# One pair of heads in eight is clipped, squared and summed on ScalarE, and a copy of scores stands ahead of the joint root

## The reference, cut to what matters

```python
def entmax15(x):
    x = (x - jnp.max(x, -1, keepdims=True)) / 2.0
    xs = jnp.flip(jnp.sort(x, -1), -1)
    rho = jnp.arange(1, x.shape[-1] + 1, dtype=x.dtype)
    mean = jnp.cumsum(xs, -1) / rho
    meansq = jnp.cumsum(xs * xs, -1) / rho
    ss = rho * (meansq - jnp.square(mean))
    tau = mean - jnp.sqrt(jnp.clip((1.0 - ss) / rho, 0.0, None))
    support = jnp.sum(tau <= xs, -1, keepdims=True)
    tau_star = jnp.take_along_axis(tau, support - 1, -1)
    return jnp.square(jnp.clip(x - tau_star, 0.0, None))
...
for _ in range(NUM_STEPS):                       # 3
    scores = jnp.einsum('bhsd,hnd->bhsn', xi, K) * beta
    w = entmax15(scores)
    xi = jnp.einsum('bhsn,hnd->bhsd', w, V)
```

## Time and profile before

| | us |
|---|---|
| median of 3 runs | 1895.13 |
| fastest and slowest of them | 1890.72, 1898.94 |
| the profiled execution, its own time | 1889.23 |
| its span, first to last instruction | 1887.4 |
| the Hopfield stage within the span | about 700 to 1382 |
| one beat in the steady part | 24.3 to 25.9 |
| one beat with output products | 26.7 to 33.6 |

### The profile page before, as it was taken

The page is one execution under the profiler, slowest core; times in us unless marked ns, Lnnn a source line. Parts: engine busy times, 40 slices in busy tenths (PEclk is TensorE's granted clock), DMA queues, the critical chain, the costliest instruction groups (busy, mean ns, idle before and its releaser), DMA issues. The chain is left out here.

```text
span 1887.4 us, 31938 instructions
## 1 busy us (share of the span) xinstructions
PE 1669.1 (88%) x10554; PEld 1156.6 (61%) x10554; DVE 1469.5 (78%) x3080; ACT 1234.6 (65%) x2769; POOL 699.6 (37%) x1326
## 2 busy tenths in 40 slices
PE   4959899999999888788889997888886899997999
PEld 3537544444444577577768886677764455545888
DVE  7767789999997268999997969999446789826655
ACT  3633477888777534788986768888652588865322
POOL 2001222222222215666675646666232111224632
PEclk9979799999999899888889999989987799988999
DMA  3464143233330100000000000000038223110000
GB/s 123 140 217 68 35 75 86 52 59 69 69 69 2 45 1 1 1 1 1 1 1 1 1 1 1 1 1 1 1 105 191 44 54 67 36 58 18 13 12 23
DMA packets 36996, 82.27 MB, mean 44 GB/s; under 512 B 9952, under 2 KB 12384, under 8 KB 35936
## 3 DMA queue, kind: packets, MB, share of 16 engines
q1 hardware_dynamic: 36192, 78.65, 17.0%
q10 hardware_dynamic: 640, 1.57, 0.4%
HBM read 52.53 MB, written 27.26 MB: 42 GB/s over the span
## 5 line engine op out<-in xcount | busy, mean ns | idle before, releaser
L1167 ACT ACTIVATE probs<-pss 128x512 f32<-128x512 f32 (+3 forms) x1152 | 481.6, 495 | 129.0 <-PE pss L1130 127.9
L873 DVE TENSOR_REDUCE negmax<-px 128x2 f32<-128x1024 f32 (+2 forms) x480 | 508.5, 1113 | 45.0 <-PE px L855 42.1
L1730 POOL TENSOR_SCALAR rp<-sw,tau 128x256 f32<-128x256 f32 x720 | 343.0, 512 | 7.1
L1234 POOL TENSOR_SCALAR_AFFINE_SELECT probs<-probs 128x512 f32<-128x512 f32 x192 | 120.8, 637 | 506.1 <-ACT probs L1167 506.1
L1130 PE MATMUL pss<-queries,keys 64*128 64x512 f32 (+3 forms) x1152 | 295.9, 396 | 5.6 <-ACT probs L1167 4.3
L855 PE MATMUL px<-keys,queries 63*128 63x512 f32 (+3 forms) x1152 | 266.3, 418 | 10.5 <-DVE negmax L873 10.5
L1130 PEld LDWEIGHTS pss<-queries,keys 64*128 64x128 f32 x1152 | 167.5, 191 | 152.5 <-ACT probs L1167 134.7
L1144 PE MATMUL po<-probs,vals 128*32 128x512 f32 (+3 forms) x2304 | 248.7, 508 | 0.4 <-POOL probs L1234 0.2
L1585 PE MATMUL pss<-again,sw 128*128 128x256 f32 x1024 | 248.9, 402 | 0.0
L1887 DVE BATCH_NORM_STATS2 st<-rp 128x6 f32<-128x512 f32 x360 | 229.6, 675 | 0.9 <-POOL rp L1730 0.9
L1585 PEld LDWEIGHTS pss<-again,sw 128*128 128x128 f32 x1024 | 206.6, 206 | 29.9
(11 more groups left out here) (375 smaller groups left out, 2548.1 us busy)
## 6 DMA issues: line engine op xcount, KB each, us to landing
queries<-rec_q SPq DMA_DIRECT2D x92, 128.0 KB, 3.6
keys<-rec_k SPq DMA_DIRECT2D x92, 128.0 KB, 3.6
queries<-rec_q SPq DMA_DIRECT2D x92, 64.0 KB, 3.4
keys<-rec_k SPq DMA_DIRECT2D x92, 64.0 KB, 3.4
rec_q<-fs SPq DMA_DIRECT2D x16, 256.0 KB, 4.2
rec_k<-fs SPq DMA_DIRECT2D x16, 256.0 KB, 4.4
rec_q<-vals SPq DMA_DIRECT2D x16, 256.0 KB, 3.0
rec_k<-vals SPq DMA_DIRECT2D x16, 256.0 KB, 3.6
```

The source lines that it names most:

```text
L873: return e.tensor_reduce(out, from_px, X_AXIS, ALU.max, negate=True)
L1167: e.activation(tl.probs[arg][:, w, :], tl.pss[scores % 3][:, 512 - width:512], ACT.Exp).then_inc(self.exp_made, 1)
L1730: x = e.tensor_scalar(self.rp[rp % 6][:, :, h], self.view(g, q)[:, h, :], -BIG, self.tau[r][:, 2 * q + h:2 * q + h + 1], ALU.min, ALU.max)
```

## The change

One pair of heads per round, pair 0 (`WHOLE` = 1), gets its two sums on ScalarE: for each of its two heads one ACTIVATE clips 256 scores and adds them up on the way (`accum_out`, into the place where `bn_stats` would have put the mean), and a second squares the result and adds that up (into `z`). Pair 1 is clipped on ScalarE and read by VectorE as before. `BY_ACT` falls from 3 to 2, so GpSimd clips pairs 2 to 7, six instead of five. VectorE has 7 `bn_stats` per round instead of 8, waits for the totals (`totals_made`) at the start of the first and of the joint step, and scales the totals by 1/256 in one small instruction of each. The ring `ra` shrinks from 7 buffers to 5. In ScalarE's order the copy `c` now stands ahead of the joint root `J`, and the first root `r` ahead of a cut and a square.

```diff
-    BY_ACT = 3
-    ACT_ORDER, PE_ORDER = "Jcdtttstsrt2ss1ttastsbss0", "ttttatbtttxcdR"
+    WHOLE, BY_ACT = 1, 2
+    ACT_ORDER, PE_ORDER = "cJdtttsrtst2ss1ttastsbss0", "ttttatbtttxcdR"
...
+        def totals(g, r):
+
+            nonlocal whole
+            self.wait_negated(e, g, r)
+            par = (g + 1 + r) % 2
+            if whole:
+                e.wait_ge(self.totals_made, whole)
+            for h in range(2):
+                e.activation(self.ends_at[h][:], self.view(g, 0)[:, h, :], ACT.Relu, bias=self.negated(g, r)[:, h:h + 1],
+                             accum_out=self.st[par][:, r, 0, 3 * h + 1:3 * h + 2]).then_inc(self.clipped, 1)
+            for h in range(2):
+                e.wait_ge(self.clipped, 2 * (whole // 2) + h + 1)
+                e.activation(self.square[h][:], self.ends_at[h][:], ACT.Square,
+                             accum_out=self.z[par][:, r, h:h + 1]).then_inc(self.totals_made, 1)
+            whole += 2
...
-                for q in range(self.BY_ACT):
+                for q in range(self.WHOLE, self.BY_ACT):
                     relus(g, r, q, ra)
                     ra += 1
+                totals(g, r)
...
-    def first_step(self, e, g, step, read_a, read_p):
+    def first_step(self, e, g, step, read_a, read_p, totals):
...
+        e.wait_ge(self.totals_made, totals)
+        step(e.tensor_scalar(m[:, whole], m[:, whole], 1.0 / NM, None, ALU.mult))
         at = step(e.tensor_tensor(m[:, by_pool], m[:, by_pool], neg[:, by_pool], ALU.add))
...
-        e.scalar_tensor_tensor(z, m2, 256.0, st[:, :, 2], ALU.mult, ALU.add).then_inc(self.first_asked, 1)
+        e.scalar_tensor_tensor(z[:, parts], m2[:, parts], 256.0, st[:, parts, 2], ALU.mult,
+                               ALU.add).then_inc(self.first_asked, 1)
...
-    def joint_step(self, e, beat, step, read_a, read_p):
+    def joint_step(self, e, beat, step, read_a, read_p, totals):
...
+        e.wait_ge(self.totals_made, totals)
+        step(e.tensor_scalar(m[:, :, whole], m[:, :, whole], 1.0 / NM, None, ALU.mult))
...
         def moments(g, r, between):
             st = self.st[(g + 1 + r) % 2][:, r]
-            pool, act = range(self.BY_ACT, self.PAIRS), range(self.BY_ACT)
+            pool, act = range(self.BY_ACT, self.PAIRS), range(self.WHOLE, self.BY_ACT)
```

27 lines of the change are left out of this document (17 added, 10 removed).

## The result

| | us |
|---|---|
| before, median of 20 runs on the same chips | 1893.59 (1885.73 to 1898.94) |
| after, median of 20 runs | 1899.53 (1892.53 to 1908.0) |
| ratio | 1.0033, 95% interval 1.0021 to 1.0046 |
| the same changed kernel in a later set of runs (`after_again`) | 1900.01; ratio 1.0048 (1.0029 to 1.0067) |
| profiled execution of after, its own time | 1899.79 |

They are not the quotient of the two medians and can differ from it by 0.1%.

A forecast was written before the change was run, and what follows sets the result against it. The loop of ScalarE's chain plus TensorE matmuls was taken to bound steady beats, VectorE close behind. Steady -0.4, c ahead of J +4.4, filling +1.2, emptying -1.0 gave +4.2 us; on the 1895.1 median, 1899.3 us, range 1888 to 1911.

The forecast's parts named there:

- s: Cost of adding up per ACTIVATE on ScalarE: 0.10 us taken, bounds 0 and 0.21; a round +0.12 us.
- The square of 256: ScalarE's ACTIVATE squaring 256 scores: claimed to go at 0.265 us before the cost of adding up.
- rival of the dear sum: ScalarE rounds 2 and 1: adding up near 0.21 us lengthens steady beats by 1.12; sum +15.6, 1910.7 us; chance 0.24.
- counterpart at s = 0: Steady beats if adding up costs nothing: a round -0.28 us, sum about -6 us; range end 1893.
- The loop: ScalarE's cuts, squares, clipping of rounds 2 and 1, TensorE's last turn, scores c and d, copy of d: 23.99 us.
- VectorE's hold on the steady beats: VectorE's thresholds delay ScalarE's cuts by 3.2 us in 15 beats, the most a faster VectorE could give.
- forecast -0.4: Sum over 15 steady beats: ScalarE's longer rounds cost 2.2 and 0.6 us, against 3.2 no longer held by VectorE.
- GpSimd: Six pairs clipped, VectorE waits for rp; its loop 23.0 to 23.9 us, still below the loop through ScalarE.
- c ahead of J: Three beats where c waits for the output product: J and the cuts come later, 1.3 + 1.3 + 1.75, +4.4 us.
- Fill: Second beat, J queued behind c, thresholds at 751.7 in place of 750.6, plus GpSimd's longer round: +1.2 us.
- Tail: Beat of 1294.8, no scores left: 1.5 of VectorE's 2.25 us hold falls away, output products take part back: -1.0 us.
- a fallen clock in the product beats: Rival: TensorE's clock falls in three beats with products, up to +8 us on top of +4.2, 1907; chance 0.07.

The follow-up runs named there:

- vector_spared: Kernel before with pair 2's bn_stats left out each round, a copy of pair 0's six numbers in its place: 1880.58 us, ratio 0.9953.
- r_early_only: Kernel before with only the first root r moved one cut and one square earlier: 1885.34 us, ratio 0.9975.
- r_late: Changed kernel with the first root r back behind the second square, c still ahead of J: 1895.64 us, ratio 1.0026.
- no_adding_up: Changed kernel without accum_out totals, pair 0 taking pair 1's sums: 1895.04 us, ratio 1.002.
- c_first_only: Kernel before with only copy c moved ahead of the joint root J: 1895.98 us, ratio 1.0024.
- experiment 11: The run r_late: changed kernel with the first root r back behind the second square: 1895.64 us, ratio 1.0026.
- plain_out_of_the_loop: Kernel before's J-first order, r early; ScalarE clips two plain pairs in rounds 2 and 1, one whole and three plain in round 0: 1880.78 us, ratio 0.9932.
- three_pairs_and_whole: Changed kernel with BY_ACT 3: ScalarE clips one whole and two plain pairs, GpSimd five: 1947.78 us, ratio 1.0305.
- c_first_where_free: Changed kernel with J ahead of c in the second beat and four product beats, c ahead of J elsewhere: 1891.96 us, ratio 1.0001.
- j_first: Changed kernel with the joint root J ahead of copy c again in every beat: 1893.55 us, ratio 1.0014.

## Why the prediction was right, and where it was not

**The price of adding up (right).** s was taken at 0.10 from the pace of a small root, with bounds 0 and 0.21. It is 0.09. No row tied a root to a total, so that the two are so close is luck; the bounds were the sound part. The square of 256 was put too low, 0.265 for 0.31; it had been worked out as a difference of two others that read PSUM, and this one reads SBUF, which may be the reason; no run separates it. Together a round costs +0.16 and not +0.12. The estimates worked out from the figures of the Trainium skill (ScalarE: Activation LUTs, What ACT_TABLE_LOAD costs), 0.400 and 0.306, agree with the 0.40 and 0.31 that the rows show for clip and square. The rival of the dear sum fell with this. (Its counterpart at s = 0 was added up wrongly: 9 x 2 x -0.28 + 0.6 - 3.2 is -7.6 and not -6. That moves the 1893 to about 1892, inside the stated range.) The Trainium skill's rule to clip on VectorE (ScalarE: Activation LUTs, Rules for kernel authors) was not put to a test: no run here clips there.

**The loop (right).** It said: cuts, squares, two rounds, last turn, c and d, copy of d, 23.99 us in the earlier trace rows, and the thresholds behind it. The floor is 23.87 (`vector_spared`), and the rest follows from the length of a round: 23.87 + 2 x 0.16 = 24.19, measured 24.19 to 24.30 in eleven of fourteen steady beats; 23.87 + 2 x (0.16 + 0.81) = 25.8 with one more pair, measured 25.9 where the clock held. The second of these decides: a loop through GpSimd is 24.2 us long too (below), but with one more pair on ScalarE GpSimd has one less.

**VectorE's hold on the steady beats (term too small).** The prediction added up ScalarE's waits for the thresholds, 3.2 us in 15 beats, and called this the most that a faster VectorE could give. `r_early_only` took 6.2 us off 14 steady beats, `vector_spared` 8.0. A wait at one place shows only what is left of a delay when it gets there. The prediction counted ScalarE's waits for turns, 2.5 us, as TensorE's own; in `vector_spared`, where only VectorE was relieved, they are gone from all fourteen beats. TensorE's clock stood higher there as well (0.98 in the first seven beats, 0.86 before), so it is not shown how much of them was VectorE's doing at first hand; and of the 8.2 us the waits for thresholds are 3.6 and those for turns 2.6 in these fourteen beats, so that some 2 us stand in neither. The right measure was the beat itself against its floor, (171.9 + 170.5) / 14 - 23.87 = 0.59 us a beat, 8.2 in all. It did no harm here, because the whole pair gave back 14 x 0.32 = 4.5 of it: steady beats came out 2.0 us better (2.9 in the second profile), forecast -0.4 in one more beat.

**GpSimd (right in kind, its loop put too short).** Twelve clippings take 5.7 to 5.9 us and VectorE waits for `rp`, 0.25 twice in a beat; less than the 0.5 to 1 us that was foretold. A wait that was not foretold is the larger one, 0.8 us for the one plain pair of ScalarE at the start of round 1, whose clipping follows two squares. In `r_late` the steady beats are as long, and VectorE stands before L1820 instead. VectorE's timeline from the start of round 1 to the thresholds:

```profile
1164.15 0.69 DVE L1909 BATCH_NORM_STATS2 st<-ra 128x6 f32<-128x512 f32 x1 [0.83 <-ACT ra L1642]
1164.76 2.46 DVE L1913 BATCH_NORM_STATS2 st<-rp 128x6 f32<-128x512 f32 x4
1167.48 0.69 DVE L1913 BATCH_NORM_STATS2 st<-rp 128x6 f32<-128x512 f32 x1 [0.26 <-POOL rp L1749]
1168.40 0.69 DVE L1913 BATCH_NORM_STATS2 st<-rp 128x6 f32<-128x512 f32 x1 [0.23 <-POOL rp L1749]
...
1178.50 0.17 DVE L1892 SCALAR_TENSOR_TENSOR neg<-step,neg 128x32 f32<-128x32 f32 x1
```

GpSimd's timeline of that beat, its start behind the thresholds and its round 1:

```profile
1154.58 0.20 POOL L1738 TENSOR_SCALAR tau<-neg 128x16 f32<-128x16 f32 x1 [4.50 <-DVE neg L1892]
...
1162.70 5.67 POOL L1749 TENSOR_SCALAR rp<-sw,tau 128x256 f32<-128x256 f32 x12
```

Between these rows GpSimd has no pause of more than 0.1 us, and behind 1168.40 VectorE has none. So there is a third loop: thresholds, GpSimd's rounds 2 and 1, VectorE, next thresholds. From the end of the thresholds at 1154.49 to the next at 1178.67 it takes 24.18 us, as long as ScalarE's. The thresholds stand 0.10 us before the cuts here, and in eight of the fourteen steady beats of this profile 0.03 to 0.04 us, which is what they show in the kernel before in beats that they hold. In `after_again` it is 0.23 to 0.74 us, in beats of the same length. The prediction had VectorE with GpSimd at 23.0 to 23.9 us. That was too short, and did no harm because ScalarE's loop is as long; `no_adding_up` ran into it at 24.1.

**c ahead of J (right, place and size).** Forecast +4.4 in three beats: +1.3, +1.3, +1.75. Measured are 4.7 us; `c_first_only` alone has them, +0.05, +1.8, +1.4 and +1.4 in its four product beats. TensorE has three gaps before the first turn, 1.20, 1.20 and 4.65 for 2.88 before.

**Fill (small miss).** +1.2 forecast, +1.9 and +2.2 measured. c waits 8.01 us for its scores with J behind it. `c_first_only` accounts for 1.5 of it.

**Tail (failed step, wrong sign).** The step said that VectorE's hold of 2.25 us at the cuts would shrink, -1.0. It shrank by half a microsecond (to 1.78), and the whole tail became 2.4 to 4.9 us longer. r had been moved ahead of a square, and I costed it at 0.1 us in each of six beats, from steady beats, where its request had always come before. In the tail the request comes late (row of L1664 in experiment 11): ScalarE stands 2.04 us at r with the second square, the clipping and the turns behind it. `r_late` moves r back and nothing else, and the beat is short again. How much of the loss is the wait itself and how much the lower clock in that beat stays open (experiment 11).

**State beats (not in the prediction).** With a whole pair the two beats together take 53.0 to 56.8 us in seven profiles and 52.4 in one (`plain_out_of_the_loop`; `three_pairs_and_whole`, whose every beat is longer, is left aside). In the five without one they take 51.5 to 52.3. Beat by beat, c and d take 7.07 us in all ten state beats without a whole pair, and 7.97 to 9.64 us in ten of the sixteen with one; `plain_out_of_the_loop` and `c_first_where_free` have none of these. One row of TensorE's timeline each, c and d in the first of the two beats: before, after, after again, and `r_late`.

```profile
964.09 7.07 PE L1585 MATMUL pss<-again,sw 128*128 128x256 f32 x32
```

```profile
961.51 8.76 PE L1587 MATMUL pss<-again,sw 128*128 128x256 f32 x32
```

```profile
964.40 9.64 PE L1587 MATMUL pss<-again,sw 128*128 128x256 f32 x32
```

```profile
960.46 7.07 PE L1587 MATMUL pss<-again,sw 128*128 128x256 f32 x32
```

Their beats took 25.87, 27.79, 29.04 and 26.32 us; in the second state beat of `r_late` c and d took 9.57 us and the beat 29.00. So some 0.4 us of such a beat is the longer rounds (26.32 - 25.87), and 1.5 to 2.7 us is c and d running partly at the 1.2 GHz level. The prediction had looked for a fallen clock in the product beats, where it stayed at 1.00 until the last gap, the one of 4.65 us. In the state beats TensorE stands still before the turn of the states, just ahead of c. Which pause tips it was not isolated: there the rows differ little (idle 1.27 us in the kernel before, 1.24 after, with 0.34 and 0.63 at the turn ahead of it; the second state beat of the kernel before has 1.24 and 0.65 and no fall). That the fall comes only with a whole pair, and not always, is what these profiles show, with it in round 0 alone too (27.2 each); how, stays open. In `three_pairs_and_whole` the same fall of c and d reached the steady beats.

**The parts do not add.** On the kernel before, c first costs 5.0 us and r early gains 5.6; the whole pair on top of r early (`j_first` against `r_early_only`, same chip) costs 8.2. r early is a gain while VectorE holds the beat and a loss of 4.4 when it no longer does. In the profiles of after and of after again the missed costs are +3.8 and +5.0 (state beats), +5.9 and +3.4 (tail, against the -1.0), 0.9 and 1.3 (fill and product beats together), and the steady beats give back 1.6 and 2.5 more than forecast. Added before rounding, that is +9.0 and +7.3 on top of the forecast +4.2, or the 13.2 and 11.5 us by which the stage is longer. The medians say +5.9 and +10.2. For the first, 4.4 us of the difference may be that the profiled execution of before lay that far under its median; how the state beats and the tail fall in executions without a profile can't be seen, and that part stays open. So the forecast time was met partly because it had been put on a median of 1895.1, while before stood at 1893.6 and 1889.8 in the sets that it was measured beside.

## What to carry to other kernels

When two loops through different engines are within 3% of each other, relieving the one that holds makes the other the bound at once: find that floor first (here by sparing VectorE and changing nothing else), then move work out of that loop too, not only off the busiest engine. Measure a hold by the beat's length over its floor, not by the waits at its last station; and where no wait is left, look at how long before its use a result arrives, since pauses of an engine are not yet room. An instruction that is moved ahead costs nothing only where what it waits for is early in every beat; look at the fill, the tail and the beats with another make-up one by one, since in them the same order meets other release times.

## What the runs showed of the hardware that was not expected

- An ACTIVATE with `accum_out` leaves a second record, `ACTIVATION_READ_ACCUMULATOR`, 0.20 us long, which delays the next start by 0.09 us. The clip before it keeps its 0.40.
- A small step of VectorE on four columns had a pace of 0.31 us in the changed kernel, between `MAX` and its successor (first row); in `r_late` the same instruction at the same place had 0.06 in the beat from 1201. What lengthens it stays open:

```profile
1169.34 0.41 DVE L1845 TENSOR_SCALAR st<-st 128x4 f32<-128x4 f32 x1
1169.65 0.18 DVE L1846 TENSOR_TENSOR st<-st,neg 128x24 f32<-128x24 f32 x1
```

- TensorE's clock held at 1.00 in product beats with a new gap of 1.2 us, and fell in beats without products whose gaps had hardly changed: the same 32 records at the same place of the changed kernel took 8.76 us in one execution and 9.64 us in another, and 7.07 us in `r_late`, where only r had moved.
